# A second chain of accumulating DMAs for row sums, and an earlier turn of the row maxima, in a fused attention and FFN kernel

## What is computed

```python
x = x + xattn(layernorm(x), ctx)      # 16 heads of 32
x = x + ffn(layernorm(x))             # one 512 x 512 product of values quantised to FP6 in blocks of 32

def xattn(x, context):
    xn, cn = layer_norm(x, g1, b1), layer_norm(context, g2, b2)
    q, k, v = xn @ Wq.T, cn @ Wk.T, cn @ Wv.T           # in heads
    attn = softmax(q k^T / sqrt(32), axis=-1)           # over the 2048 context tokens
    return (attn @ v) @ Wo.T + bo
```

## Time and profile before

| | |
|---|---|
| median of 3 runs | 5109.6 us (5100.05 to 5109.68) |
| the profiled execution: device time | 5101.1 us |
| its span, first to last instruction | 5099.3 us |
| mean granted TensorE clock | 0.975 |
| PE matmul busy | 92% |
| DVE busy | 67% |
| ACT busy | 56% |
| POOL busy | 54% |
| DMAs issued by POOL (merges) | 192, of 1 MB |

### The profile page before, as it was taken

How to read it: one execution, slowest core, us unless ns; L and a number is a source line. 1 busy time by engine, 2 the same in 40 slices (tenths; PEclk the granted TensorE clock), 3 DMA queues, 4 the chain that set the end, 5 groups by cost and what they waited for, 6 DMA issues and landing times.

```text
span 5099.3 us, 65944 instructions
## 1 busy us (share of the span) xinstructions
PE 4692.1 (92%) x25616; PEld 1365.5 (27%) x25616; DVE 3424.9 (67%) x3983; ACT 2842.2 (56%) x5128; POOL 2762.7 (54%) x1218
## 2 busy tenths in 40 slices
PE   5999889998899988999889998899988999889998
PEld 2322242222422224222242222422224222242222
DVE  4688557885478854788547885478844788447883
ACT  3477534775347753477534774457744567345773
POOL 2267643666336663376633766346762467525665
PEclk9999999999999999999999999999999999999999
DMA  5223422234322343232432324323333223332232
GB/s 178 64 59 73 122 88 62 59 67 121 94 55 59 67 122 97 52 67 60 123 96 53 72 59 118 100 53 67 67 113 104 54 59 70 113 105 57 60 67 71
DMA packets 173787, 413.39 MB, mean 81 GB/s; under 512 B 26833, under 2 KB 100881, under 8 KB 146594
## 3 DMA queue, kind: packets, MB, share of 16 engines
q0 software_dynamic: 27648, 201.34, 19.7%
q1 hardware_dynamic: 145826, 207.83, 13.2%
HBM read 110.98 MB, written 21.01 MB: 26 GB/s over the span
## 4 chain that ended last, share of the span: by engine, by line
PE 72%; SPq 7%; DVE 6%; ACT 6%; DMA 4%; POOL 3%; issue 2%; ACTq 0%; DVEq 0%; POOLq 0%
PE banks L895 18%; PE banks L905 17%; PE banks L814 11%; PE banks L873 9%; PE banks L808 8%; PE banks L929 7%; SPq L285 4%; DVE max_parts L544 3%; ACT region L704 3%; SPq L311 3%; DMA queries_stacked<-max_rows 2%; PE banks L785 2%; POOL wkT_wvT_wqT L384 1%; DMA region<-in_x 1%; ACT values L770 1%
## 5 line engine op out<-in xcount | busy, mean ns | idle before, releaser
L544 DVE TENSOR_REDUCE max_parts<-banks 128x2 f32<-128x1024 f32 x2048 | 2410.0, 1220 | 597.1 <-PE banks L873 595.1
L704 ACT ACTIVATE region<-banks 128x512 f32<-128x512 f32 x4096 | 2214.4, 595 | 831.9 <-PE banks L895 791.3
L384 POOL TENSOR_TENSOR wkT_wvT_wqT<-region 128x2048 f32<-128x2048 f32 x320 | 1475.4, 4611 | 1274.1 <-ACT region L704 1160.0
L895 PE MATMUL banks<-queries_stacked,keys_stacked 98*128 98x512 f16 x4096 | 1261.4, 387 | 92.1 <-DMA queries_stacked<-max_rows 58.9
L905 PE MATMUL banks<-region,values 128*32 128x512 f32 x8192 | 1104.2, 611 | 7.6
L873 PE MATMUL banks<-keys_stacked,queries_stacked 33*128 33x512 f16 x4096 | 662.2, 387 | 43.1 <-DMA keys_stacked<-region 34.4
L895 PEld LDWEIGHTS banks<-queries_stacked,keys_stacked 98*128 98x128 f16 x4096 | 277.8, 97 | 1433.1 <-ACT region L704 1267.6
L814 PE MATMUL banks<-region,wkT_wvT_wqT 128*128 128x512 f16 x2304 | 580.0, 394 | 70.2 <-POOL region L373 45.5
L562 DVE RECIPROCAL row_sums_inverse<-row_sums_inverse 128x128 f32<-128x128 f32 x256 | 235.2, 934 | 399.9 <-ACT row_sums_inverse L721 399.9
L535 DVE SCALAR_TENSOR_TENSOR region<-banks,region 128x512 f16<-128x512 f32 x192 | 132.5, 690 | 439.4 <-ACT region L689 438.5
L814 PE MATMUL banks<-wkT_wvT_wqT,region 128*128 128x512 f16 x1536 | 378.0, 389 | 1.9 <-DVE region L535 1.8
(11 more groups left out here) (75 smaller groups left out, 2779.2 us busy)
## 6 DMA issues: line engine op xcount, KB each, us to landing
wkT_wvT_wqT<-wkT_wvT_wqT POOLq DMA_DIRECT2D x128, 1024.0 KB, 7.0
wkT_wvT_wqT<-sums POOLq DMA_DIRECT2D x64, 1024.0 KB, 7.0
keys_stacked<-region SPq DMA_DIRECT2D x768, 64.0 KB, 2.0
region<-in_x SPq DMA_DIRECT2D x24, 1024.0 KB, 7.8
wkT_wvT_wqT<-weights_split SPq DMA_DIRECT2D x8, 3072.0 KB, 18.2
queries_stacked<-region SPq DMA_DIRECT2D x384, 64.0 KB, 2.0
region<-in_context SPq DMA_DIRECT2D x16, 1024.0 KB, 6.3
values<-in_context SPq DMA_DIRECT2D x16, 1024.0 KB, 6.0
```

The costliest lines, as they stand in the source:

```text
L384: e.tensor_tensor(SUMS[dst], PR[i], PR[i + 1], ALU.add).then_inc(s_pr, 1)
L544: e.tensor_reduce(mpart[:, buf, :, a, t, c], MXB[parity], AX.X, ALU.max).then_inc(s_mxd, 1)
L704: e.activation(PR[u % 4][:, j * HALF:j * HALF + HALF], score_bank(kt, j)[0], ACT.Exp, scale=SCALE).then_inc(s_ex, 1)
L895: e.matmul(dst, KA[0:STR, ds(ka + (j * C + (u + 1) * P), P)], QA[0:STR, ds(qa[j], HALF)], start=True, stop=True).then_inc(s_st, 1)
```

## The change

Seven things are edited.

1. A second chain of accumulating DMAs (`merge_late`) adds pairs 5 and 6 onto pair 4, in SUMS[4], in every unit but the last of a batch. Its first DMA is issued directly after merge 2, after pair 5. Its second is issued after pair 6, once the first has landed.
2. The buffers of the pair sums rotate with period 3 (`buffers`), and POOL's waits are rearranged to match.
3. PE makes four row sums per unit: tile 14 in step 15, and in the next unit's steps 0, 2 and 4 tile 15, the first merged buffer and the second merged buffer. The last unit of a batch keeps six, all in its step 15.
4. `between` is called between the outputs and scores 2 and 3 of a step, so the maxima are turned in the middle of step 13. ACT copies them halfway through tile 14's exponentials.
5. Three score banks are used for tiles 7 to 13 and 15; tiles 14 and 0 may run three back for their first two scores. Tile 15 waits for the maxima's copy, since they lie in bank 7. Bank 7 is cleared for row sums in step 15, not in step 14.
6. ACT's copy of the finished row sums moves from tile 5's to tile 6's exponentials.
7. SP's reload of the FFN weights waits for step 15 of the last unit instead of step 14.

```diff
--- before.py
+++ after.py
@@ -161,9 +161,15 @@
         def score_bank(tile, j):
-            if 6 <= tile < KT - 1:
-                return bank((7, 4, 5)[(4 * (tile - 6) + j) % 3]), 3
-            return bank(4 + j % 2), 2
+            if 7 <= tile < 14:
+                return bank((7, 4, 5)[(4 * (tile - 7) + j) % 3]), 3
+            if tile == 15:
+                return bank((7, 4, 5)[j % 3]), 3
+            return bank(4 + j % 2), 3 if tile in (0, 14) and j < 2 else 2
+        def buffers(n):
+            return [(0, 1, 2, 3, 4), (3, 1, 0, 2, 4), (2, 1, 3, 0, 4)][n % 3]
         s_w = sem("weights_loaded")
         s_wf = sem("full_projection_weights_loaded")
@@ -202,6 +208,7 @@
         s_pv = sem("pv_steps_done")
         s_pr = sem("exponentials_paired")
         s_acc = sem("pairs_merged")
+        s_ac2 = sem("late_pairs_merged")
         s_po = sem("unit_outputs_done")
         s_oc = sem("unit_outputs_copied")
         s_on = sem("unit_row_sums_copied")
@@ -315,9 +322,8 @@
                 for row, src in ((bo_all, bo), (wb_all, wb)):
                     e.dma_start(row, src.rearrange("(a n) -> a n", a=1).broadcast_to([P, D])).then_inc(s_xl[0], 16)
-                e.wait_ge(s_pv, b * (NU * KT) + NU * KT + 3)
+                e.wait_ge(s_pv, b * (NU * KT) + NU * KT + 4)
                 e.dma_start(SUMS[4], wd_dram).then_inc(s_fl, 16)
-                e.wait_ge(s_pv, b * (NU * KT) + NU * KT + 4)
                 for h in range(2):
                     e.dma_start(X1[:, 4 * h:4 * h + 4, :], xb[:, h]).then_inc(s_xl[h], 16)
@@ -383,35 +389,52 @@
                             i = 2 * (p % 2)
                             e.tensor_tensor(SUMS[dst], PR[i], PR[i + 1], ALU.add).then_inc(s_pr, 1)
-                        here, other = n % 2, 1 - n % 2
+                        first, one, two, three, second = buffers(2 * g + q)
+                        end = g == G - 1 and q == 1
+                        late = b * (2 * NU - 2) + 2 * (2 * g + q)
                         def merge(i, p, src):
                             e.wait_ge(s_pr, n * 7 + 2 + p + 1)
                             if i > 0:
                                 e.wait_ge(s_acc, (3 * n + i) * 16)
-                            e.dma_start(SUMS[here], SUMS[src], accum_op=ALU.add).then_inc(s_acc, 16)
-                        e.wait_ge(s_pv, n * KT + (3 if g + q > 0 else 4))
-                        pair(0, here)
-                        e.wait_ge(s_pv, n * KT + 4 + 2)
-                        pair(1, other)
-                        merge(0, 1, other)
-                        e.wait_ge(s_pv, n * KT + 4 + 4)
-                        pair(2, 2)
+                            e.dma_start(SUMS[first], SUMS[src], accum_op=ALU.add).then_inc(s_acc, 16)
+                        def merge_late(i, p, src):
+                            e.wait_ge(s_pr, n * 7 + 2 + p + 1)
+                            if i > 0:
+                                e.wait_ge(s_ac2, (late + i) * 16)
+                            e.dma_start(SUMS[second], SUMS[src], accum_op=ALU.add).then_inc(s_ac2, 16)
+                        e.wait_ge(s_pv, n * KT + 4)
                         if n > 0:
                             e.wait_ge(s_acc, 3 * n * 16)
-                        pair(3, 3)
-                        merge(1, 2, 2)
-                        pair(4, other)
+                        pair(0, first)
+                        if g + q > 0:
+                            e.wait_ge(s_ac2, (late - 1) * 16)
+                        pair(1, one)
+                        merge(0, 1, one)
+                        e.wait_ge(s_pv, n * KT + 4 + 3)
+                        pair(2, two)
+                        if g + q > 0:
+                            e.wait_ge(s_ac2, late * 16)
+                        pair(3, three)
+                        merge(1, 2, two)
+                        e.wait_ge(s_pv, n * KT + 4 + 5)
                         if g + q == 0:
                             e.wait_ge(s_fs, 16)
                             if b > 0:
                                 e.wait_ge(s_ff, b * TT)
-                        pair(5, 4)
-                        merge(2, 3, 3)
-                        pair(6, 2)
+                        pair(4, second)
+                        e.wait_ge(s_acc, (3 * n + 1) * 16)
+                        pair(5, one)
+                        merge(2, 3, three)
+                        if not end:
+                            merge_late(0, 5, one)
+                        pair(6, two)
+                        if not end:
+                            merge_late(1, 6, two)
                 e.wait_ge(s_xl[0], b * 48 + 48)
                 def out_bias(i):
                     if i == 4:
@@ -724,12 +747,14 @@
                         for u in range(4):
                             kt = 4 * k + u + 1
                             exps(m, g, kt // 4, kt % 4,
-                                 (lambda: row_sums(m - 1, KT + 4)) if kt == 5 and n > 0 else None)
+                                 (lambda: row_sums(m - 1, KT + 5)) if kt == 6 and n > 0 else None)
                     exps(m, g, KT // 4 - 1, 1)
-                    exps(m, g, KT // 4 - 1, 2)
-                    if not end:
+                    def turned():
                         e.wait_ge(s_mr, 64 * (m + 1))
                         turned_maxima(n + 1, 1 - q)
+                    exps(m, g, KT // 4 - 1, 2, None if end else turned)
                     exps(m, g, KT // 4 - 1, 3)
                     def outputs():
@@ -880,7 +905,7 @@
                     e.matmul(turn, nmax[:, buf, :], ident[:, :], start=True, stop=True).then_inc(s_mt, 1)
                 def step(m, ex, ka, qa, v, u, tile, row=None, after=None, sums=(), end=False, between=None, scores=True,
-                         weigh=True, fresh=None, closing=False):
+                         weigh=True, fresh=None, closing=False, turning=True):
                     if row:
                         count, *piece_of = row
                     if after:
@@ -890,8 +915,10 @@
                         if scores:
                             dst, back = score_bank(tile, j)
                             e.wait_ge(s_ex, ex + (u + 1) * J + j + 3 - back)
-                            if back == 3 and tile == 6 and j == 0:
+                            if tile == 7 and j == 0:
                                 e.wait_ge(s_on, m + 1)
+                            if tile == 15 and j == 0 and turning:
+                                e.wait_ge(s_mc, m + 2)
                             e.matmul(dst, KA[0:STR, ds(ka + (j * C + (u + 1) * P), P)],
                                      QA[0:STR, ds(qa[j], HALF)], start=True, stop=True).then_inc(s_st, 1)
@@ -913,6 +940,8 @@
                         mm = outputs()
                         if end:
                             mm.then_inc(s_po, 1)
+                    if between:
+                        between()
                     score(2)
                     score(3)
                     if not weigh:
@@ -929,8 +958,6 @@
                             mm = e.matmul(LB[HD * j:HD * j + HD, :], ones[:, :], src[:, ds(j * HALF, HALF)],
                                           start=False, stop=closing and i == len(sums) - 1, skip_group_check=True)
                     mm.then_inc(s_pv, 1)
-                    if between:
-                        between()
                 def clear(bank, left, count):
                     e.wait_ge(left, count)
@@ -954,38 +981,42 @@
-                    def late(m):
-                        return [(PR[3], None), (SUMS[m % 2], (s_acc, 48 * (m + 1))), (SUMS[4], (s_pr, m * 7 + 8)),
-                                (SUMS[2], (s_pr, m * 7 + 9))]
-                    def quad(k, ex, ka, v, rows, carried=((),) * 4):
+                    def quad(k, ex, ka, v, rows):
                         for u in range(4):
-                            step(m, ex, ka, qa, v, u, 4 * k + u + 1, rows[u], sums=carried[u], closing=u == 3)
+                            t = 4 * k + u
+                            sums = []
+                            if g + q > 0:
+                                if t == 0:
+                                    sums = [(PR[3], None)]
+                                if t == 2:
+                                    sums = [(SUMS[buffers(2 * g + q - 1)[0]], (s_acc, 48 * m))]
+                                if t == 4:
+                                    sums = [(SUMS[4], (s_ac2, 16 * (b * (2 * NU - 2) + 2 * (2 * g + q))))]
+                            step(m, ex, ka, qa, v, u, t + 1, rows[u], sums=sums, closing=t == 4)
                     clear(OB, s_oc, m + 1)
-                    quad(0, *at(0, 0, ng, nq, not end), *([[[c] for c in late(m - 1)]] if g + q > 0 else []))
+                    quad(0, *at(0, 0, ng, nq, not end))
                     for k in range(1, K3):
                         quad(k, *at(k, k, ng, nq, not end))
                     ex, ka, v, rows = at(K3, J - 1, g + 1, q, not last)
```

(17 more changed lines are left out.)

## The result

The changed kernel takes **5446.64 us** as a median of 4 runs (5443.97 to 5451.49), the kernel before 5105.65 beside it (5100.05 to 5109.68): a ratio of **1.067, 95% interval 1.0651 to 1.0688**. The profiled executions differ by 5449.7 - 5099.3 = 350.4 us of span, the mean granted TensorE clock fell from 0.975 to 0.933. The forecast was 5406 us, in a range of 5065 to 5470.

The account below looks back on a forecast made before the run. PE's instructions bound steps 15 to 12, the chain of turn, copy, DMA issues and landing steps 13 and 14. Terms -21 + 283 + 5 + 6 + 2 + 22 = +297 us gave 5398 profiled, 5406 as a median; range 5065 to 5470.

Parts of the forecast that it names:

- the forecast case: Rows' DMAs wait for both merges at steps 13 and 14: 5406 us as a median, chance 0.67.
- (c), steps 13 and 14: Rows wait for merge 2 and late merge 0; step 15 starts 11.9 us behind step 13, +4.3 in 48 boundaries.
- the rows' bursts only behind: Sign of being right: DMA engines full for 10 us on end, the maxima rows' bursts only after that.
- (c), the clock: PE's clock falls after the 6.3 us wait for the rows: +1.6 us per boundary, bounds 0 and 3.2.
- (a): Row sums in steps 0 to 4: -0.98 us each, +0.54 for two-bank waits; net -0.44 x 48 = -21 us.
- (b): Turn moved to mid-step 13: alone, step 15 would start 6.53 us behind step 13 instead of 7.61, -1.08.
- (d): POOL's two more DMA issues of 0.87 us around pair 6: covered; last merge lands before step 4 needs it.
- (e): Small ones: clear in step 15 +5 us, last unit's wait for tile 15's exponentials +6, unit 0's tile 6 +2.
- (f): SP's FFN weights' reload goes just ahead of X1, delaying POOL at a batch's end: +2.8 x 8 = +22 us.
- Rival 1: All four rows' DMAs slip between merge 2 and late merge 0: 5071 us, faster; chance 0.22.
- Rival 3: Gains and losses cancel, rows landing at about 7.3 us: 5110 us, within 0.2%; chance 0.05.
- Rival 2: Rows get through, but DVE's normalisation meets POOL's pair 1 and takes 4.62 us, not 0.69: 5247 us; chance 0.06.

Follow-up runs that it names:

- e4: Changed kernel with two of the four rows' DMAs issued from ACT's queue instead of SP's: 5325.71 us.
- e1: Changed kernel with late merge 0 issued behind pair 6 instead of directly behind merge 2: 5297.37 us.
- e2: Changed kernel without its second chain: five row sums in the next unit's steps 0 to 4, turn still mid-step: 5265.05 us.
- e10: Kernel before with only merge 2 moved behind pair 6 (old place in a batch's last unit): ratio 1.0145 to the kernel before.
- e7: e2 with merge 2 issued behind pair 6: 5127 us.
- e11: e10 with merge 2 also held on POOL until the next unit's rows have landed: 0.9909 of the kernel before.
- e8: e7 with the fifth row sum back in step 14 and tile 15 in two banks: missed its expected 5050 to 5070 us by 65 us or more.
- e5: Changed kernel with SP's X1 input loads issued before the FFN weights' reload instead of behind it: 5458.31 us.
- e12: Changed kernel with one late merge, merge 2 behind pair 6 and held until the rows land, last unit as in the kernel before: 5032.51 us, ratio 0.9860.

## Why the prediction held, point by point

The direction, the mechanism and the place were right: the forecast case came true, and the time fell 41 us above it, inside the range (which stops at 5470, though its own working goes up to 5478).

**(c), steps 13 and 14: right in size, half right in mechanism.** 11.9 predicted, 11.91 measured; POOL's issues and SP's first came where they were put, SP's four took 4.51 us instead of the 3.12 that the step used, but the last was still issued (1043.84) before merge 2's end (1044.6). The step said that the rows wait for the end of both merges. They waited for the end of merge 2, but passed one by one inside late merge 0, so its sign "the rows' bursts only behind" did not come true. The last one was through at 1049.1, the merge at about 1049.6, so both readings give 11.9, and that the number came out so close is in part luck; another number of DMAs would have told them apart, and e4 did, with two queues and 10.1 us. The Trainium skill's rule ("DMA: Bandwidth & Descriptors", section "Queues, rings and completion order"), by which a DMA engine goes round the queues at each packet's end, fits what was seen in the second merge, if the 8 KB pieces of the trace (0.64 us each, 8 of them per engine) are its packets, and not the 5 us without a burst in the first; the prediction had taken a whole merge for one packet, which fits the first and not the second.

What differs between the two can be narrowed down, if a row is called due 1.28 us behind its issue, an estimate from the earlier trace rows. Where the first row was due 2.2 us into a moving merge (e1, e2) or 3.5 (before), its burst came at the merge's end, about 5.0 us behind its first packet, in all of the 48 places; rows that already stood in line when a merge began, or were due with its first packet (the late merge here, the fourth row of e10), took turns with it from 0.6 us on. No run varied this alone, and why it is so stays open.

**(c), the clock: the term that was mis-sized.** The step put it at 1.6 us a boundary, from one row after a wait of 2.28 us. Measured are 2.30 - 0.10 (the clearing) = 2.20 in step 15 and, behind it, in steps 0 to 4 of units 1 to 6, 0.17 more where they should take 0.44 less, 0.61: together **2.8**. Two forms occur: step 15 of 5.2 to 5.4 us, where the clock comes back within it, as above, in 23 of the 48 places, and of 6.86, where it does not and the loss reaches into the steps behind, in 25:

```profile
2569.36 1.03 PE L922 MATMUL banks<-queries_stacked,keys_stacked 98*128 98x512 f16 x2 [6.41 <-DMA queries_stacked<-max_rows]
...
2576.22 1.03 PE L922 MATMUL banks<-queries_stacked,keys_stacked 98*128 98x512 f16 x2
```

(2.8 - 1.6) x 48 = 58 us is the whole of the shortfall of the sum (297 against 350, 53 us); the other terms together came out 5 us below their forecast. The upper bound of 3.2 had held it. The mean granted clock went to 0.933 and not to 0.95, which fits that. The row that the step read was one of 3 in the trace of the kernel before in which the clock fell, and there it came back within the step each time.

**(a)** right: 16.58 us in steps 0 to 4 against 16.6, where the clock is up. e7 bears out both of its numbers: its five sums instead of three should cost 2 x 0.98 less the 0.54 of the two-bank waits, 1.42, and its steps 0 to 4 take 18.0 over units 1 to 6, 1.4 more.

**(b)** wrong as a saving: "6.53 behind step 13, if alone". The 4.20 us from issue to PE were read in the kernel before, where merge 2 is in the way; without one they are 3.48. So there are two values, 5.7 with no merge (e7) and 7.6 with merge 2 (e2), and never 6.53. The turn's move is worth nothing while merge 2 stands where it does. With the merge out of the way e11 has 6.9 without the turn's move, and e7 5.7 with it; but e7 also has the fifth sum out of step 14. With the turn moved and that sum kept there, e8 has 6.8 and PE hardly waits any more. So the move alone is worth 0.1, and 1.2 only together with the sum's 0.98, which e7 pays in another step. PE's arrival, 5.56 predicted, is 1043.90 - 1038.39 = 5.51.

**(d)** right: PE waits for no late merge in steps 2 and 4, though one lands in 11.4 us.

**(e)** the clearing, right (3.81 in e7 against 3.71 in e8, e11 and, with the clock up, before). The last unit costs 1.5 us instead of 0.7: from its last scores (step 14) to the first matmul behind the row sums are 10.07 us (2668.41 to 2678.48) instead of 8.6.

**(f)** right in place, too large by a third. X1 does come later: POOL's wait for it grew from 92.2 to 118.7 us over 8 batches, and e5, which takes the reload out of the way, brings POOL's first use of it forward by 2.5 us. At the end of the tail (the last matmul with the FFN weights, counted from the last unit's step 14) the changed kernel is at 85.7 us, the kernel before at 82.1. Of these 3.6 us 1.5 are (e), so 2.1 a batch are left, 17 us instead of 22. e5 gives back 1.2 of them and e12, with the last unit and the reload as in the kernel before, nearly all (82.3).

**The rivals.** Rival 1 (rows get through) fell at once: nothing passes merge 2. Rival 3 (gains and losses cancel) needed the rows at about 7.3. Rival 2 (DVE's normalisation meets POOL) needed pair 1 to come first. DVE's normalisation took a median of 0.69 us, and started 0.32 us ahead of pair 1, the 0.3 that the step had left:

```profile
1064.93 0.69 DVE L592 TENSOR_TENSOR queries_stacked<-queries_stacked,row_sums_inverse 128x512 f32<-128x512 f32 x1
```

One thing the prediction read in its rows, that in the kernel before the rows wait for merge 2's end, and drew nothing from: e11 takes that wait away, 0.8 us a unit in steps 13 and 14, and is 47 us faster.
